# A four-layer tower on one core: three of the edge sort's exchange distances on VectorE's shuffle, the second attention's inverse sums on ScalarE, and its next norm's statistics taken inside it

## Time and profile before

| what | value |
|---|---|
| median of three runs | 6085.68 us |
| the profiled execution's own time | 6076.21 us |
| its span | 6074.5 us |
| PE busy in the span | 4905.7 us (81%) |
| DVE busy | 4695.5 us (77%) |
| ACT busy | 2461.6 us (41%) |
| POOL busy | 2671.5 us (44%) |
| attn1's block, from its first maxima to its last addition | 914.33 to 1496.10 us |
| the norm behind it | to 1534.97 us |
| layer 1's experts, with the last slots of the sort | to 1705.49 us |

### The profile page before, as it was taken

The page is one execution under the profiler, slowest core; times in us unless marked ns, Lnnn a source line. Parts: engine busy times, 40 slices in busy tenths (PEclk is TensorE's granted clock), DMA queues, the critical chain, the costliest instruction groups (busy, mean ns, idle before and its releaser), DMA issues. The chain is left out here.

```text
span 6074.5 us, 108916 instructions
## 1 busy us (share of the span) xinstructions
PE 4905.7 (81%) x39862; PEld 3331.9 (55%) x39929; DVE 4695.5 (77%) x8591; ACT 2461.6 (41%) x4417; POOL 2671.5 (44%) x3019
## 2 busy tenths in 40 slices
PE   5567968886637999998799999999990298967998
PEld 3463226664424666665677777777770027852452
DVE  7896988897696888887588888888883467767657
ACT  4453433333434666666233333343340143222332
POOL 0000010000324675886667777777774301015557
PEclk8787989998668999999799999999995599978999
DMA  0300000111312110000122222222220000030252
GB/s 18 84 1 6 8 23 28 30 32 39 109 50 36 19 28 17 2 2 9 28 41 43 46 44 44 43 44 43 43 44 15 5 1 4 3 74 18 67 133 44
DMA packets 269133, 208.06 MB, mean 34 GB/s; under 512 B 139498, under 2 KB 242835, under 8 KB 267571
## 3 DMA queue, kind: packets, MB, share of 16 engines
q1 hardware_dynamic: 195806, 145.14, 8.5%
q0 software_dynamic: 72912, 57.02, 6.1%
q10 hardware_dynamic: 12, 0.39, 0.0%
HBM read 113.55 MB, written 69.40 MB: 30 GB/s over the span
## 5 line engine op out<-in xcount | busy, mean ns | idle before, releaser
L3514 PE MATMUL edges_bank<-part_room,hot_room 128*128 128x512 f32 x6656 | 1528.8, 391 | 78.2 <-ACT XT L3537 57.5
L3514 PEld LDWEIGHTS edges_bank<-part_room,hot_room 128*128 128x128 f32 x6656 | 1249.3, 188 | 357.8 <-ACT XT L3537 69.7
L3493 POOL DMA_INDIRECT XT<-gat_node_table,edges_idx x1216 | 1203.2, 989 | 392.5 <-issue 311.8
L3537 ACT COPY XT<-edges_bank 128x512 f32<-128x512 f32 x832 | 474.8, 597 | 657.6 <-PE edges_bank L3514 562.9
L3632 DVE COPY_PREDICATED XT<-edges_tabs_p,XT 128x1024 f32<-128x1024 int32 (+7 forms) x768 | 576.9, 751 | 38.3 <-DVE edges_acc_s L3681 7.1
L3613 DVE TENSOR_SCALAR hot_room<-edges_lanes,edges_nodes 128x512 fp32r<-128x512 f16 (+1 forms) x768 | 351.1, 518 | 172.0 <-PE edges_bank L3514 86.2
L505 POOL TENSOR_TENSOR X<-H,ln_f_mean 128x1024 f32<-128x1024 f32 x5 | 11.4, 2279 | 913.2 <-DVE ln_f_shift L542 913.2
L1837 ACT ACTIVATE GT<-attc_sc,attc_nm 128x256 f32<-128x256 f32 x1024 | 399.5, 480 | 32.0 <-DVE attc_nm L1915 32.0
L1915 DVE TENSOR_REDUCE attc_nm<-attc_sc 128x4 f32<-128x1024 f32 x256 | 312.8, 1222 | 110.1 <-PE attc_sc L1756 110.1
L1851 ACT ACTIVATE GT<-attc_sct 128x1024 f32<-128x1024 f32 x256 | 262.1, 1024 | 305.3 <-PE attc_sct L1767 305.2
L1756 PE MATMUL attc_sc<-XT,attc_tT 64*128 64x256 f32 x2048 | 296.5, 409 | 43.8 <-ACT GT L1837 43.8
(11 more groups left out here) (850 smaller groups left out, 10203.5 us busy)
## 6 DMA issues: line engine op xcount, KB each, us to landing
gat_states<-GT SPq DMA_DIRECT2D x32, 768.0 KB, 3.3
XT<-gat_node_table,edges_idx POOLq DMA_INDIRECT x1216
edges_lanes<-gat_places SPq DMA_DIRECT2D x128, 128.0 KB, 3.0
expert_pairs<-in_L_ffn_W_dram SPq DMA_DIRECT2D x48, 256.0 KB, 4.1
edges_lanes<-gat_places SPq DMA_DIRECT2D x64, 160.0 KB, 3.2
XT<-XT SPq DMA_DIRECT2D x32, 256.0 KB
XT<-XT SPq DMA_DIRECT2D x64, 128.0 KB
XT<-XT SPq DMA_DIRECT2D x128, 64.0 KB
```

The source lines that it names most:

```text
L3493: nc.gpsimd.indirect_dma_start(out=rows[:, k, c, :], out_offset=None, in_=q.t_table, in_offset=bass.IndirectOffsetOnAxis(ap=idx[:, k, c:c ...
L3514: m = nc.tensor.matmul(banks[t][:], hot[:, (k * GROUPS + j) % 2, b, t, :], parts[:, p, b].rearrange("p u c -> p (u c)"), start=b == 0 and ...
L3537: nc.scalar.copy(fetched[:, (k * GROUPS + j) % 2, t].rearrange("p u c -> p (u c)"), banks[t][:]).then_inc(fetched_in, 1)
```

## The change

`attn1` gets a function `invert` on ACT: Ln of the spread sums, in place, then Exp with scale -1. DVE's `normalize` is parted: `spread_sums` stays at a block's end, the multiplication moves one block later, behind the maxima. One of the two slots of the sort now stands ahead of the maxima, the other behind the multiplication. A function `measure` takes bn_stats of the two tiles of the block that has been added. In ffn1 the norm becomes `known=True`. In the sort, bits 2, 3 and 4 (SHUFFLED) send no DMA; each merge slot of theirs begins with a stream_shuffle of 128 x 1024 into the third room. Below, the renaming of semaphores is cut.

```
--- before.py
+++ after.py
...
@@ -2203,9 +2203,17 @@
                         act.wait_ge(normed, b - 1)
                     nc.scalar.copy(o[:, b % 2], o_p).then_inc(o_moved, 1)
 
-                for i in range(-AHEAD - 1, B):
+                def invert(b):
+                    act.wait_ge(spread, b + 1)
+                    nc.scalar.activation(total[:], total[:], ACT.Ln).then_inc(logged, 1)
+                    act.wait_ge(logged, b + 1)
+                    nc.scalar.activation(total[:], total[:], ACT.Exp, scale=-1.0).then_inc(inverted, 1)
+
+                for i in range(-AHEAD - 1, B + 1):
                     if 0 <= i < B:
                         exps(i)
+                    if 0 <= i - 1:
+                        invert(i - 1)
                     if i + AHEAD + 1 < B:
                         move_queries_keys(i + AHEAD + 1)
                     if 0 <= i < B:
@@ -2233,15 +2241,21 @@
                     v.wait_ge(s_full, b + 1)
                     vec.tensor_reduce(mx[:, b % 2].rearrange("p u s c -> p c u s"), scores_p, AX.X, ALU.max).then_inc(max_ready, 1)
 
-                def normalize(b):
+                def spread_sums(b):
                     v.wait_ge(o_moved, b + 1)
                     vec.stream_shuffle(total[:], o[:, b % 2], [ONES + n % ONES for n in range(ROWS)]).then_inc(spread, 1)
-                    v.wait_ge(spread, b + 1)
-                    vec.reciprocal(total[:], total[:]).then_inc(inverted, 1)
+
+                def normalize(b):
                     v.wait_ge(inverted, b + 1)
                     if b >= 2:
                         v.wait_ge(misc_full, b + 1 + AHEAD)
                     vec.tensor_tensor(oT[:, b % 2].rearrange("p (j u) -> p u j", u=2), o[:, b % 2], total[:], ALU.mult).then_inc(normed, 1)
+
+                def measure(b):
+                    v.wait_ge(misc_read, b + AHEAD + 3)
+                    for t in range(b * TPB, (b + 1) * TPB):
+                        m = vec.bn_stats(g.stats[:, t, :], g.H[:, t, :])
+                    return m
 
                 def move_rows(b):
                     if b >= 2:
@@ -2259,10 +2273,15 @@
                     return vec.tensor_tensor(h, h, add_p, ALU.add)
 
                 for i in range(-AHEAD - 1, B + 1):
+                    hidden = HIDDEN["attb"] // B if 0 <= i + AHEAD < B else 0
+                    for _ in range(hidden // 2):
+                        g.order.vector(v)
                     if 0 <= i + AHEAD < B:
                         maxima(i + AHEAD)
-                        for _ in range(HIDDEN["attb"] // B):
-                            g.order.vector(v)
+                    if 0 <= i - 1:
+                        normalize(i - 1)
+                    for _ in range(hidden - hidden // 2):
+                        g.order.vector(v)
                     v.wait_ge(misc_full, i + AHEAD + 2)
                     if 0 <= i + AHEAD < B:
                         move_rows(i + AHEAD)
@@ -2273,8 +2292,10 @@
                         m = add(i - 1)
                     m.then_inc(misc_read, 1)
                     if 0 <= i < B:
-                        normalize(i)
-                v.wait_ge(misc_read, B + AHEAD + 1)
+                        spread_sums(i)
+                    if 0 <= i - 2:
+                        measure(i - 2)
+                link(measure(B - 1))
 
 
 def attn3(nc, g, I):
@@ -2774,7 +2795,7 @@
 
 def ffn1(nc, g, q, pairs, I):
 
-    turned_norm(nc, g, "ln_f1", g.H, keep=g.X)
+    turned_norm(nc, g, "ln_f1", g.H, keep=g.X, known=True)
     sequence_experts(nc, g, "expb", pairs, I["L1_ffn_Wr"], I["L1_ffn_br"], I["L1_ffn_b1"], I["L1_ffn_b2"], g.X, HIDDEN["expb"])
     lane_of_nodes(nc, g, q, g.order)
     layernorm(nc, g, "ln_out1", g.X, I["L1_ffn_gamma"], I["L1_ffn_beta"], add=g.H, drained=(g.order.stored, 48))
@@ -2786,6 +2807,7 @@
 NODE_BITS = 14
 LOW = TOKENS - 1
 SAMPLES = 32
+SHUFFLED, LANES = (2, 3, 4), 32
 HIDDEN = {'atta': 64, 'expa': 128, 'attb': 128, 'expb': 61}
 
 
@@ -2804,13 +2826,15 @@
         self.swapped = [st.sem(f"swapped{h}") for h in range(2)]
         self.gathered = [st.sem(f"gathered{k}") for k in range(2)]
         self.stored, self.lanes_ready, self.searched = st.sem("stored"), st.sem("lanes_ready"), st.sem("searched")
+        self.shuffled, self.shuffles = st.sem("shuffled"), 0
         row_bits, levels = ROW.bit_length() - 1, EDGES.bit_length() - 1
         self.row_bits = row_bits
         self.slots, self.parity_at = [("keys", 0, 0, n, 0) for n in range(4)], 0
         swaps = [0, 0]
 
         def exchange(h, b):
-            swaps[h] += 16 * len(self.partners(b))
+            if b not in SHUFFLED:
+                swaps[h] += 16 * len(self.partners(b))
             return swaps[h]
 
         def within(k, j):
@@ -2903,7 +2927,12 @@
             if kind == "scale":
                 m = vec.tensor_scalar(to, src, mine, None, ALU.mult)
             else:
-                v.wait_ge(self.swapped[part], swaps[0])
+                if b in SHUFFLED:
+                    self.shuffles += 1
+                    vec.stream_shuffle(other[:, cols], src[:, cols], [n ^ (1 << b) for n in range(LANES)]).then_inc(self.shuffled, 1)
+                    v.wait_ge(self.shuffled, self.shuffles)
+                else:
+                    v.wait_ge(self.swapped[part], swaps[0])
                 m = vec.scalar_tensor_tensor(src[:, cols], other[:, cols], theirs, to[:, cols], ALU.mult, ALU.min)
         m.then_inc(self.stepped, 1)
 
@@ -2918,6 +2947,8 @@
         elif kind == "within" and b == 0 and self.row_bits <= k < EDGES.bit_length() - 1:
             result, bit = 1 - parity, k - self.row_bits
         else:
+            return
+        if bit in SHUFFLED:
             return
         cols = slice(part * (ROW // 2), (part + 1) * (ROW // 2))
         sp.wait_ge(self.stepped, n + 1)
```

More of the change, by code:

```diff
@@ L2037, in attn1 @@
         names = ("loaded", "cleared", "made", "own", "ready", "biased", "qk_full", "qk_moved", "misc_full", "misc_read", "rows_ready",
-                 "s_full", "max_ready", "st_full", "prob_ready", "o_full", "o_moved", "spread", "inverted", "normed")
+                 "s_full", "max_ready", "st_full", "prob_ready", "o_full", "o_moved", "spread", "logged", "inverted", "normed")
         (loaded, cleared, made, own, ready, biased, qk_full, qk_moved, misc_full, misc_read, rows_ready,
-         s_full, max_ready, st_full, prob_ready, o_full, o_moved, spread, inverted, normed) = (st.sem(n) for n in names)
+         s_full, max_ready, st_full, prob_ready, o_full, o_moved, spread, logged, inverted, normed) = (st.sem(n) for n in names)
         rows_in = [st.sem(f"rows_in{n}") for n in range(2)]
```

11 lines of the change are left out of this document (6 added, 5 removed).

## The result

| | before | changed |
|---|---|---|
| median of four runs | 6084.51 us (6072.29 to 6087.12) | 6039.85 us (6038.82 to 6044.21) |
| profiled execution | 6076.21 us | 6044.21 us |

The ratio is 0.9943, 95% interval [0.9922, 0.9965]: faster by 0.57%.

The account below looks back on a forecast made before the run. No engine was full over the whole span; attn1 lost most to PE's waits for the maxima rows' DMAs behind the sort's copies. Terms -2 + 6 - 10.5 - 18 = -24.5 us gave a 6061 us median, range 6035 to 6086.

Parts of the forecast that it names:

- Two table loads a block: attn1 on ACT: Ln and the Exp behind it each need a table load, making ACT's chain 8.89 us a block.
- The 60 blocks: attn1, fourth maxima to the last: 533.4 us against 535.2, -2 us; loads use up the gain on DMAs and inverse.
- The stage's end: attn1's last three blocks: ACT's inverse with loads stands on the path alone; with the last bn_stats, about +6 us.
- The norm: Norm behind attn1: its 128 bn_stats move into attn1, hidden in DVE's room; -10.5 us (-11 to -9.5).
- The experts: Layer 1's experts: 16 sort slots fall from 58.5 to 40.5 us with six shuffled merges, -18 us (-24 to -7).
- Sum: Whole kernel: -2 + 6 - 10.5 - 18 = -24.5 us; 6051.7 from the profiled execution, 6061 for a median.
- Who sets 7.81: attn1's undisturbed block pace before the change, 7.81 us: put down to a ring that doesn't hold the inverse, not DVE alone.
- The ring of the maxima: attn1: cycle of maxima, PE's values, projections, turned scores, scores and maxima again, without the inverse; 7.81 us a block.
- ACT's ring: attn1: cycle of Exp, load, Ln, load, Exp, copies and PE's turned scores; 8.89 us a block, longer than 7.81.
- Rival 1: attn1: one table load serves Ln and Exp; 60 blocks in 475.6 us, sum -89, 5997 us; chance 0.11.
- Rival 2: attn1: a table switch costs 1.02 us more in the busy stream, 122 times; +124, 6185 us; chance 0.06.
- Rival 3: attn1: the 18 shuffles aren't hidden and all count, +22.5 us; 6083 us, no change; chance 0.05.

Follow-up runs that it names:

- e1: Changed kernel plus one line naming the table set with both exp and ln at the start of attn1's ScalarE block: 5975.4 us, ratio 0.9846.
- e12: Changed kernel with the exp-and-ln table set named in attn1 and four extra small Exp behind each block's Exp: 6031.0 us, ratio 0.9943.
- e11: Kernel before plus only attn1's bn_stats behind the multiplication and the norm with known statistics: 6071.2 us, ratio 1.0000.
- e3: Kernel before plus only the sort's shuffles for bits 2, 3 and 4: 6027.7 us, ratio 0.9924.
- e8: Changed kernel with both of a block's sort slots ahead of the maxima: 6057.9 us, ratio 0.9975.
- e7: Changed kernel with the exp-and-ln table set named in attn1 and the Exp of the turned scores done twice a block: 6131.7 us, ratio 1.0088.

## Why the prediction came out, step by step

- **Two table loads a block** (ring 8.89): right, 8.91, and e1 and e12 show that the loads are the cause. The Trainium skill ("ScalarE: Activation LUTs", Table sets) gives natural_log_exp_and_others as the set with both exp and ln; that e1, where it is named, has no load left agrees. The same section counts one load for an Ln and an Exp behind it; the changed kernel, where the set isn't named, has two for each such pair, 128 in all. The same page's drain of about 1380 ns (What ACT_TABLE_LOAD costs) is in no row here (a function begins 0.01 to 0.02 us behind its load), and e12 excludes it.
- **The 60 blocks** (-2): -0.7, and -1.4 in the first three blocks.
- **The stage's end** (+6, bounds +3 to +9): +9.0. I priced three inverses; there are four. Of their eight loads one begins just ahead of the last maxima (1469.04) and seven behind, and of these one, at 1493.21, is made while ACT has to wait anyway. e1 ends 9.5 us sooner.
- **The norm** (-10.5): -10.7. But "hidden in DVE's room" holds only because the loads, or the shift of the inverse, had made that room (e11).
- **The experts** (-18): -21.7 in the stage, -23.2 in the sixteen slots, in this pair of traces. Over the four traces with DMAs and the eight with these shuffles the stage takes 177.9 and 159.7 in the mean, -18.1: the sum was right. Its parts were not, and they cancel: I took 58.5 to 40.5 for the slots, where the means are 56.0 and 36.7. The shuffled merges were right, six sequences of 2.95 from start to start (1598.69 to 1604.59 for two) for 2.92. The ten others I took at 2.1 each as a mean of both clocks, plus 2 of waits, 23 in all; they took 16.0 + 1.5. PE's clock was at the half level in part of the stretch, as these windows show (stretch, its length, busy us of PE, PEld, DVE, ACT, POOL, clock, DMA share, GB/s):

```profile
1605.00:1610.00 5.00, 5.00 (x34) 3.48 (x33) 4.96 (x10) 2.05 (x5) 2.13 (x2) 0.50 0.26 65
1610.00:1615.00 5.00, 5.00 (x37) 3.50 (x35) 4.96 (x9) 2.26 (x6) 2.35 (x2) 0.58 0.18 53
1615.00:1620.00 5.00, 3.05 (x35) 2.16 (x34) 4.93 (x10) 2.60 (x8) 3.22 (x3) 1.00 0.67 197
```

  DVE is full there all the same. Two sequences at 2.95 and one at 1.60 make 2.50 each, which is PE's pace at the half level, so PE kept up. The right sum takes the waits out of the slots: 16 x 1.60 = 25.6, 6 x 1.35 = 8.1 for the shuffles, 1.5 of waits, 35.2; before, 25.6 + 26.4 for DMAs + 5.0 for PE, 57.0 of the 58.5. I had left those 5.0 in. In the eight traces with these shuffles the slots take 35.3 to 37.8 us with 0 to 1.7 us of waits for PE, in the four with DMAs 54.5 to 58.5. That the triple's pace is why PE doesn't hold DVE up is read from the windows; no run isolates it.
- **Sum** (-24.5): -25.5 between the marks. The +3 at the end and the -4 in the experts cancel, and a part of the -4 is chance. The predicted 6061 lies 21 above the median, because the sum was laid on a median 9.5 above the profiled execution, and later sets put the kernel before at 6068 to 6073. That the measured 6039.9 lies in the stated 6035 to 6086 is luck in part: the bounds -41 and +9 were laid on the profiled 6076.2, the forecast on the median, and laid on the median, too, they give 6045 to 6095, which misses it. The bounds of the terms add up to -42 and +6.5, besides.
- **Who sets 7.81** was read wrongly. I wrote that the ring doesn't hold the inverse; DVE never waits in a plain block of the kernel before, plain blocks mostly take 7.92, and statistics that take 0.26 us from their start to the next made them 8.17. The ring of the maxima is there all the same, 7.82 in e1, and hides behind nearly the same number. It did no harm, since ACT's ring was longer than either.
- **Rival 1's** mechanism (no second load) is real and needed only the line of code: its 475.6 us for the 60 blocks against 474.4 in e1. **Rival 2** has nothing for it. **Rival 3**: three blocks around a pair of shuffled merges take 9.18 + 9.67 + 7.88 against 3 x 8.91, hidden. It isn't the loads alone that hide them, as I wrote: in e1, without loads, the 60 blocks take 474.4 us against 60 x 7.82 = 469.2, so that the shuffles cost 5 us. With the inverse on DVE they show in full (e3), and with both slots ahead of the maxima 7 us of their 21 (16 x 1.31) show (e8).

## What to carry to other kernels

Before an operation is moved to ACT, list the functions that the stage alternates between and name the one table set that holds them all; a pair of loads in every block can eat the whole gain and hide behind an unchanged total. An unchanged stage time after a large edit is a reason to take the two halves apart: here +40 and -41 us stood in the same 534 us, and the shuffles alone were worth twice the whole change. Size a stretch as work plus the waits it shows, not as a mean over clock levels, and look which engine never waits: it is the one that new work lands on.

## What was not expected of the hardware

- A table load whose function waits for a semaphore is made ahead: at 1493.21 it begins behind the copy (1492.84 + 0.35), and the Ln that needs it begins at 1495.34 behind a wait of 0.85. This load ends before the sums that Ln waits for are there, and so costs nothing.
- A shuffle of 128x1024 takes 1.31 us and one of 128x256 0.42: by these two sizes 1.15 ns a column and some 0.13 fixed.
- In e7 PE waits 1.83 us ahead of L2105 in every block. In the blocks of 10.9 us the two groups behind it take 3.70 us from start to the next group's start, with a granted clock of 0.54 over the 3.70 us from 1197.93 on, near its lower level of 1.2 GHz; in those of 9.36 us they take 2.12, at 1.00. The difference of 1.58 is that between the blocks. The wait is the same in both kinds of block, so why the clock falls in one and not in the other is open.
